# Feed-forward up projection of an attention and feed-forward kernel: eight instead of six of the eleven feature tiles of a pair by seven block products, and rows copied to fp16 by GpSimd

## The reference, cut to what matters

```python
x = x + xattn(layernorm(x), ctx, ...)          # not touched
xq = act_fake_quant(layernorm(x), clip_x)      # whole numbers -128..127 times a scale
gate = einsum('bsh,ih->bsi', xq, weight_fake_quant(w_gate))   # 512 -> 1408
up = einsum('bsh,ih->bsi', xq, weight_fake_quant(w_up))       # 512 -> 1408
h = act_fake_quant(silu(gate) * up, clip_down)
x = x + einsum('bsi,hi->bsh', h, weight_fake_quant(w_down))   # 1408 -> 512
```

## Time and profile before

| | us |
|---|---|
| median of three runs | 1239.04 (1238.58 to 1240.55) |
| the profiled execution | 1239.66 |
| its span in the trace | 1237.9 |
| attention, start to the first feed-forward matmul | 0 to 783.0 |
| groups 0 and 1 | about 789 to 826 |
| the six pairs | about 826 to 1039 |
| groups 14 and 15 | about 1039 to 1078 |
| down projection | about 1082 to the end |

### The profile page before, as it was taken

One profiled execution on the slowest core, in us unless ns is written; L12 is line 12 of the kernel. 1 busy time (PEld: TensorE's weight loads), 2 busy tenths in 40 slices (PEclk: granted clock), 3 DMA queues, 4 the chain that ended last, 5 costly groups with the idle time before them and its releaser, 6 DMA issues.

```text
span 1237.9 us, 20617 instructions
## 1 busy us (share of the span) xinstructions
PE 1230.6 (99%) x7500; PEld 573.2 (46%) x7500; DVE 1052.5 (85%) x1917; ACT 858.5 (69%) x1349; POOL 381.1 (31%) x295
## 2 busy tenths in 40 slices
PE   8999999999999999999999999999999999999998
PEld 5544444444444444444444444544444444444444
DVE  7976988988988898898898868889999998888777
ACT  6888577657757757756765763468888885399760
POOL 0113343144044134224314420224444443022223
PEclk9999999999999999999999999999999999999999
DMA  8284346256254363462462483398976854199996
GB/s 315 86 255 171 95 137 209 66 159 190 79 178 152 111 191 108 120 222 69 137 228 79 119 236 131 139 289 242 278 239 228 272 183 154 47 372 414 423 426 261
DMA packets 174565, 241.74 MB, mean 195 GB/s; under 512 B 122608, under 2 KB 142080, under 8 KB 156928
## 3 DMA queue, kind: packets, MB, share of 16 engines
q1 hardware_dynamic: 174432, 240.42, 58.5%
q10 hardware_dynamic: 32, 0.01, 0.0%
HBM read 120.86 MB, written 90.57 MB: 171 GB/s over the span
## 4 chain that ended last, share of the span: by engine, by line
PE 93%; ACT 3%; DVE 2%; DMA 1%; issue 1%; SPq 1%; ACTq 0%
PE bank L2502 12%; PE po L81 10%; PE po L83 9%; PE po L82 9%; PE bank L2379 8%; PE ring L83 8%; PE ring L82 8%; PE ring L81 8%; PE bank L2384 4%; PE bank L2385 4%; PE bank L2360 3%; PE bank L2341 3%; PE ring L1257 2%; PE ring L1284 2%; DMA x<-in_x_dram 1%; ACT E L479 1%
## 5 line engine op out<-in xcount | busy, mean ns | idle before, releaser
L81 PE MATMUL ring<-yT,M 128*128 128x512 f16 x512 | 194.1, 379 | 0.0
L82 PE MATMUL ring<-yT,M 128*128 128x512 f16 x512 | 194.0, 379 | 0.0
L83 PE MATMUL ring<-yT,M 128*128 128x512 f16 x512 | 194.0, 379 | 0.0
L81 PE MATMUL po<-VW,p 128*128 128x512 f16 x480 | 182.2, 380 | 0.0
L82 PE MATMUL po<-VW,p 128*128 128x512 f16 x480 | 181.9, 379 | 0.0
L83 PE MATMUL po<-VW,p 128*128 128x512 f16 x480 | 181.9, 379 | 0.0
L494 ACT ACTIVATE p<-E 128x512 f16<-128x512 f32 x120 | 74.8, 625 | 122.7 <-DVE E L741 122.7
L414 POOL TENSOR_TENSOR esum<-E 128x512 f32<-128x512 f32 x16 | 23.4, 1462 | 409.2 <-DVE p L745 369.6
L417 POOL TENSOR_TENSOR esum<-esum,E 128x512 f32<-128x512 f32 x96 | 129.5, 1349 | 51.2 <-ACT E L483 18.4
L2502 PE MATMUL bank<-w,hb 128*128 128x512 f16 x605 | 131.3, 379 | 0.0
L1989 ACT ACTIVATE hb<-hb,hscale 128x512 int8<-128x512 f32 (+1 forms) x155 | 95.2, 709 | 16.7 <-DMA hb<-hidden 13.4
(11 more groups left out here) (389 smaller groups left out, 2492.9 us busy)
## 6 DMA issues: line engine op xcount, KB each, us to landing
xa<-x_rows_d SPq DMA_DIRECT2D x28, 1024.0 KB, 6.9
hidden<-hb SPq DMA_DIRECT2D x22, 1024.0 KB, 9.1
hb<-hidden SPq DMA_DIRECT2D x18, 1024.0 KB, 9.8
x<-in_x_dram SPq DMA_DIRECT2D x16, 1024.0 KB, 5.2
value_fold<-E SPq DMA_DIRECT2D x64, 256.0 KB, 2.5
VW<-value_fold SPq DMA_DIRECT2D x16, 1024.0 KB, 6.5
x_rows_d<-x SPq DMA_DIRECT2D x16, 1024.0 KB, 6.0
out_dram<-xa SPq DMA_DIRECT2D x11, 1024.0 KB, 11.6
```

The lines of the kernel that those rows point to most:

```text
L81: nc.tensor.matmul(out, a_hi, b_hi, start=first, stop=False)
L82: nc.tensor.matmul(out, a_hi, b_lo, start=False, stop=False)
L83: return nc.tensor.matmul(out, a_lo, b_hi, start=False, stop=last)
```

## The change

Joint tiles of a pair are now 0, 1, 3, 4, 6, 7, 9, 10, single ones 2, 5, 8. Where two joint tiles follow each other (also from tile 10 to tile 0 of the next pair), `first` and `seed` of the next go ahead of `fourth` of the one at hand (`ahead`). GpSimd copies rows to fp16, one row block at a time (`round_row`), from group 5 on; VectorE's `round_x` is left for groups 1 to 4. Odd groups have a buffer of their own (`xq_odd`). The weight sums are in eight instructions over four tiles each, where there were four over six. The rows to normalise are at other tiles, and VectorE's order in a pair is a new one.

```diff
-    JOINT = tuple(range(0, FT, 2))
+    JOINT = tuple(i for i in range(FT) if i % 3 != 2)
+    SINGLE = tuple(i for i in range(FT) if i % 3 == 2)
     NJ, NS = len(JOINT), FT - len(JOINT)
     ALL_J, ALL_S = NJ * len(PAIRS), NS * len(PAIRS)
-    joint = lambda p, i: NJ * (p - 1) + i // 2
-    TAKEN = ("seed", "third", "silu_a", "fourth", "silu_b")
+    joint = lambda p, i: NJ * (p - 1) + JOINT.index(i)
+    ahead = lambda K: 0 < K < ALL_J and (K % NJ == 0 or JOINT[K % NJ] - 1 in JOINT)
...
+    def order_of_takes():
+
+        taken = []
+        for K in range(ALL_J):
+            if not ahead(K):
+                taken.append(("seed", K))
+            taken.append(("third", K))
+            if K > 0:
+                taken.append(("silu_b", K - 1))
+            taken.append(("silu_a", K))
+            if ahead(K + 1):
+                taken.append(("seed", K + 1))
+            taken.append(("fourth", K))
+        taken.append(("silu_b", ALL_J - 1))
+        return {take: n + 1 for n, take in enumerate(taken)}
+
+    TAKEN = order_of_takes()
+    taken_joint = lambda what, K: TAKEN[what, K]
...
+    BY_POOL = 5
+    xq_of = lambda g: xq_apart if g == 2 else xq_odd if g >= BY_POOL and g % 2 else xq[:]
...
+    xq_odd = spare16[:, SUMS_T + SUMS_W:SUMS_T + SUMS_W + TT * D].rearrange("p (t d) -> p t d", t=TT)
...
+    def rows_of_pair(p):
+
+        early = {6: (2 * p + 4, 0), 9: (2 * p + 4, 3)}
+        late = {1: (2 * p + 3, 1), 3: (2 * p + 3, 2), 4: (2 * p + 3, 3), 6: (2 * p + 4, 1), 7: (2 * p + 4, 2), 9: (2 * p + 5, 0)}
+        if p == 1:
+            early[1] = (2 * p + 3, 0)
+        return [{i: row for i, row in rows.items() if row[0] < NG} for rows in (early, late)]
...
         def turn(g):
-            sp.wait_ge(x_rounded, g)
+            if g < BY_POOL:
+                sp.wait_ge(x_rounded, g)
+            else:
...
+            third_tiles = lambda half, c0, n: half.rearrange("p c (i n) -> p c i n", n=P)[:, c0:c0 + 2, n:FT:3]
+            of_them = lambda k, n: wsum[:, k, :, n:len(JOINT):2]
+            for n in range(2):
+                nc.gpsimd.tensor_tensor(of_them(2, n), third_tiles(wg, 0, n), third_tiles(wu, 0, n), ALU.subtract).then_inc(w_summed, 1)
+                nc.gpsimd.tensor_tensor(of_them(0, n), third_tiles(wu, 0, n), third_tiles(wu, 2, n), ALU.add).then_inc(w_summed, 1)
...
+        def round_row(g, t):
+
+            pool.wait_ge(x_normed, TT * (g - 1) + t + 1)
+            if g > BY_POOL:
+                pool.wait_ge(x_turned[g % 2], 64 * ((g - 1) // 2))
+            nc.gpsimd.tensor_copy(xq_of(g)[:, t], ints_of(g)[:, t]).then_inc(rows_rounded, 1)
+
         over_partitions(0)
         sum_weights()
         for p in PAIRS:
+            early, late = rows_of_pair(p)
             for i in JOINT:
                 add_fourth(p, i)
+                if i in early:
+                    round_row(*early[i])
+                if i in late:
+                    round_row(*late[i])
                 joint_hidden_b(p, i)
...
         for p in PAIRS:
+            early, late = rows_of_pair(p)
             for i in JOINT:
-                seed(p, i)
+                if not ahead(joint(p, i)):
+                    seed(p, i)
                 keep_third(p, i)
+                if i - 1 in SINGLE:
+                    single_silu(p, i - 1, 1)
                 if i > 0:
-                    single_silu(p, i - 1, 1)
-                if joint(p, i) > 0:
-                    joint_silu_b(p if i > 0 else p - 1, i - 2 if i > 0 else JOINT[-1])
-                if p == 1:
-                    early, late = {2: (2 * p + 3, 0), 4: (2 * p + 3, 2)}, {2: (2 * p + 3, 1), 4: (2 * p + 3, 3)}
-                else:
-                    early, late = {2: (2 * p + 3, 1), 4: (2 * p + 3, 3)}, {0: (2 * p + 3, 0), 2: (2 * p + 3, 2)}
-                early.update({6: (2 * p + 4, 0), 8: (2 * p + 4, 2)})
-                late.update({6: (2 * p + 4, 1), 8: (2 * p + 4, 3)})
-                if i in early and early[i][0] < NG:
+                    joint_silu_b(p, JOINT[JOINT.index(i) - 1])
+                elif p - 1 in PAIRS:
+                    joint_silu_b(p - 1, JOINT[-1])
+                if i in early:
                     normalise_row(*early[i])
                 joint_silu_a(p, i)
-                if i < JOINT[-1]:
+                if i + 1 in SINGLE:
                     single_silu(p, i + 1, 0)
-                if i in late and late[i][0] < NG:
+                if i in late:
                     normalise_row(*late[i])
+                if i + 1 in JOINT:
+                    seed(p, i + 1)
+                elif i == JOINT[-1] and p + 1 in PAIRS:
+                    seed(p + 1, 0)
                 keep_fourth(p, i)
...
             if p - 1 in PAIRS:
+                pair_reach(p - 1, 8)
+                joint_hidden_a(p, 0)
                 pair_reach(p - 1, 7)
-                single_hidden(p - 1, 9, 1)
-                joint_hidden_a(p - 1, 10)
+                pair_reach(p - 1, 9)
+            else:
+                joint_hidden_a(p, 0)
+                round_x(4)
+            cross(p, 1)
+            single_hidden(p, 2, 0)
+            if p - 1 in PAIRS:
                 pair_reach(p - 1, 6)
-                cross(p, 0)
-                pair_reach(p - 1, 9)
-            single_hidden(p, 1, 0)
-            joint_hidden_a(p, 0)
-            round_x(2 * p + 2)
+                joint_hidden_a(p, 1)
+                pair_reach(p - 1, 10)
+            else:
+                reach(1, 9)
+                joint_hidden_a(p, 1)
+                reach(1, 10)
+            cross(p, 3)
+            single_hidden(p, 2, 1)
+            pair_reach(p, 0)
+            joint_hidden_a(p, 3)
             if p - 1 in PAIRS:
-                pair_reach(p - 1, 8)
-            single_hidden(p, 1, 1)
-            cross(p, 2)
-            if p - 1 in PAIRS:
-                pair_reach(p - 1, 10)
                 join_pair(p - 1)
             else:
-                reach(1, 9)
-                reach(1, 10)
                 join_group(1)
-            single_hidden(p, 3, 0)
-            joint_hidden_a(p, 2)
             pair_reach(p, 1)
-            pair_reach(p, 0)
-            single_hidden(p, 3, 1)
             cross(p, 4)
-            if p > 1:
-                round_x(2 * p + 3)
-            pair_reach(p, 3)
-            if p == 1:
-                round_x(2 * p + 3)
+            pair_reach(p, 2)
             single_hidden(p, 5, 0)
             joint_hidden_a(p, 4)
-            pair_reach(p, 2)
+            pair_reach(p, 3)
+            cross(p, 6)
             single_hidden(p, 5, 1)
-            cross(p, 6)
             pair_reach(p, 5)
-            single_hidden(p, 7, 0)
             joint_hidden_a(p, 6)
             pair_reach(p, 4)
+            cross(p, 7)
+            single_hidden(p, 8, 0)
+            joint_hidden_a(p, 7)
             if p + 1 in PAIRS:
                 sum_x(p + 1, 0)
                 sum_x(p + 1, 1)
-            single_hidden(p, 7, 1)
-            cross(p, 8)
+            cross(p, 9)
+            single_hidden(p, 8, 1)
             if p + 1 in PAIRS:
                 sum_x(p + 1, 2)
-            single_hidden(p, 9, 0)
-            joint_hidden_a(p, 8)
+            joint_hidden_a(p, 9)
+            cross(p, 10)
             if p + 1 in PAIRS:
                 sum_x(p + 1, 3)
-            cross(p, 10)
-        pair_reach(PAIRS[-1], 7)
-        single_hidden(PAIRS[-1], 9, 1)
-        joint_hidden_a(PAIRS[-1], 10)
-        pair_reach(PAIRS[-1], 6)
+            joint_hidden_a(p, 10)
+            if p + 1 in PAIRS:
+                cross(p + 1, 0)
         for i in range(FT):
+            if i == 1:
+                pair_reach(PAIRS[-1], 9)
             hidden(2, i)
             if i == 0:
-                pair_reach(PAIRS[-1], 9)
-                pair_reach(PAIRS[-1], 8)
+                for m in (8, 7, 6):
+                    pair_reach(PAIRS[-1], m)
             else:
                 reach(2, i - 1)
             if i == 1:
-                pair_reach(PAIRS[-1], JOINT[-1])
+                pair_reach(PAIRS[-1], 10)
             if i == 2:
                 join_pair(PAIRS[-1])
...
             for i in JOINT:
                 if joint(p, i) == 0:
                     pe.wait_ge(x_turned[0], 64 * p)
-                if joint(p, i) == 0 or i > 0:
+                if not ahead(joint(p, i)):
                     joint_first(p, i)
                 joint_third(p, i)
                 if joint(p, i) == 0:
                     up(1, FT - 1, ("up",))
+                if i - 1 in SINGLE:
+                    single_product(p, i - 1, 2)
                 if i > 0:
-                    single_product(p, i - 1, 2)
-                if joint(p, i) > 0:
-                    joint_close(p if i > 0 else p - 1, i - 2 if i > 0 else JOINT[-1])
-                if 0 < i < JOINT[-1]:
-                    single_product(p, i - 1, 3)
+                    joint_close(p, JOINT[JOINT.index(i) - 1])
+                elif p - 1 in PAIRS:
```

(58 more changed lines are left out.)

15 lines of the change are left out of this document (8 added, 7 removed).

## The result

| | before | after |
|---|---|---|
| median us | 1239.55 (1238.58 to 1240.55, 4 runs) | 1252.56 (1251.32 to 1255.72, 4 runs) |
| ratio, 95% interval | | 1.011 (1.0098 to 1.0123) |
| profiled execution, span | 1239.66, 1237.9 | 1255.72, 1253.9 |

The change makes the kernel 13.0 us slower. The profiled execution of after is its slowest, 3.2 us above its median; I come back to that.

A forecast was written before the change was run, and what follows sets the result against it. TensorE, 99% busy, was the bound: matmuls and old gaps removed (-5.2, -0.7) and new waits (6.4, 1.3, 0.7, 2.35, 2.6, 0.75, 1.5) sum to +9.7 us. Forecast 1248.5 us; range 1238 to 1256, own 1244 to 1253.

The forecast's parts named there:

- TensorE as the bound, and the matmuls: TensorE is busy 99% of the span; 160 matmuls a pair instead of 164 save 5.2 us.
- ScalarE's rows in tiles 6 and 9: Two rows ahead of keep_fourth make TensorE's close wait 0.64 us, ten times: 6.4 us.
- Where joint tiles adjoin: Borders between neighbouring joint tiles, where TensorE waits for VectorE's and ScalarE's results; priced place by place.
- Tile 10: first of the next pair waits for joint_silu_b, fourth for cross: 0.25 us, at five borders 1.3 us.
- pair 6: Its tile 10 has no first between second and fourth, so TensorE waits 0.7 us once.
- tile 1: VectorE's two maxima ahead of cross delay TensorE 0.5 us; at five borders 2.6 us.
- Tile 0: GpSimd's two copies delay joint_silu_b of 10; TensorE waits 0.47 us, at five borders 2.35 us.
- rival 3: GpSimd becomes a bound, a copy taking 1.28 us or more: 1255.6 us, chance 0.14.
- The load: Load of group 2p+5 lands after ScalarE wants its first row in tile 9: 0.3 us, five pairs, 1.5 us.
- Pair 1's start: Waits in tile 0 (0.25) and tile 1 (0.5, round_x(4) in the maxima's place): 0.75 us together.
- The first: Rival: the waits do not form and the count of matmuls decides, 1233.2 us; chance 0.14.
- The second: Rival: only ScalarE's rows cost (6.4 us), the other waits are hidden: +0.5, 1239.5 us; chance 0.09.

The follow-up runs named there:

- the first experiment: The changed kernel, but ScalarE normalises row (2p+5, 0) in tile 1 of the next pair instead of tile 9: 1246.59 us, ratio 1.006.
- the three together: The changed kernel with (2p+5, 0) in the next pair's tile 1, (2p+4, 1) behind keep_fourth, tile 9's maximum behind cross: 1242.34 us, ratio 1.0023.
- the copies alone: The kernel before with only GpSimd's row copies to fp16 from group 5 on and a buffer for odd groups: 1241.74 us, ratio 1.0021.
- the casts given back: A version with tile 8's products moved into tiles 9 and 10, VectorE's order mended, but VectorE making all casts, GpSimd none: 1266.51 us, ratio 1.022.

## Why the prediction was right

The measured 1252.56 us lies within the forecast's own range (1244 to 1253), at its upper end and 4.1 us above its point, 1248.5. The mechanism was right; some sizes were not, and two agreed by luck.

**TensorE as the bound, and the matmuls.** Right: 24 matmuls fewer, and the loss and the gain of every version is read as waits of TensorE.

**ScalarE's rows in tiles 6 and 9.** 6.4 forecast, 6.2 measured, and the two experiments that move one row each take the wait to 0.10. That rests on rows of before alone: differences of starts on one engine could be added up over seven instructions to 0.01 us.

**Where joint tiles adjoin.** Tile 10 1.3 (1.35), pair 6 0.7 (0.71), tile 1 2.6 (2.2: the chain to `fourth` is 4.22 for 4.18, but a close of 0.10 already delays TensorE on its side). Tile 0 2.35 (1.7). Its chain came out: from `keep_fourth` of 9 (899.18) to `joint_silu_b` of 10 (904.09) are 4.91 us, forecast 4.9. But TensorE waits 0.33 and not 0.45: the forecast added 0.12 for the close's own latency to a wait that covers it.

That two copies take 1.67 us there (901.06 to 902.73), for 1.6 forecast, is luck. A copy alone takes 0.61 and lets the next start after 0.55; two of those would by the forecast's own sum (up to 0.63 each) have made nothing wait. The second takes 1.15, beside a `sum_x`, and a price for GpSimd and VectorE getting in each other's way is what the forecast had put at nothing. GpSimd's copies into one of the two buffers (count, then minimum, median, maximum in ns; the other 20 have 604/612/1075):

```profile
L1886 POOL CAST hb<-xa x24: 607/614/1158, 836.7 to 1039.0; 128x512 f16<-128x512 int8 x24
```

The forecast took 0.8, between the bounds 0 and 1.28.

The Trainium skill, GPSIMD Engine Reference, section "Engine selection", with its one-input work roughly at line rate, gave an estimate of 0.43 for it; the trace has 0.61 alone, nearly half as much again, and a mean of 0.73.

Made twice, the copies make TensorE wait 1.80 us at a border: that is rival 3's mechanism, at the length of copies it needed (1.28). At their own length they cost next to nothing there: with one copy less in the first experiment, 0.33 of the 0.40 us stayed, since `cross` of tile 0 then makes TensorE wait.

**The load: the term that was mis-sized.** 0.3 us in five pairs was forecast, 1.5; the profiled execution has 4.8 in three. The timeline of SyncE, of the first pair and of the fourth:

```profile
847.01 6.47 SPq L1734 DMA_TRANSPOSE xqT<-hb  x4
853.53 0.58 SPq L1716 DMA_DIRECT2D xa<-x_rows_d  x1
...
961.98 5.12 SPq L1734 DMA_TRANSPOSE xa<-hb  x4
967.15 0.58 SPq L1716 DMA_DIRECT2D xa<-x_rows_d  x1
```
```profile
860.65 0.81 ACT L1927 ACTIVATE xa<-xa,row_bias,rowq 128x512 int8<-128x512 f32 x1 [1.33 <-DMA xa<-x_rows_d]
...
975.90 0.81 ACT L1927 ACTIVATE xa<-xa,row_bias,rowq 128x512 int8<-128x512 f32 x1 [1.62 <-DMA xa<-x_rows_d]
```

In the first pair four turns take 6.47 instead of 5.12, and the load lands 7.1 after its issue. In the fourth the turns are as before, and the load takes 8.75 (in the third 8.6), beside DMA engines at a share of 1.01. In the second and the fifth pair it takes 7.0 and 6.9, at shares of 0.85 and 0.87, and lands 0.1 to 0.2 us before ScalarE wants it. The stretches of the second and the fourth pair, the DMA share last but one:

```profile
890.00:900.00 10.00, 9.54 (x45) 4.16 (x44) 8.19 (x11) 8.96 (x16) 7.04 (x8) 1.00 0.85 264
967.00:977.00 10.00, 8.59 (x40) 3.72 (x38) 7.40 (x10) 7.55 (x13) 6.12 (x7) 1.00 1.01 310
```
So the place was priced right to 0.5 us where the load takes its usual time. I had put one value each, 5.17 and 7.0, where the trace of before gave only a median; a wait behind two DMAs needs their spread. At its median the kernel is 3.2 us better than in this execution. That this wait and the clock behind it make the difference is argued only: the versions without the load's wait spread over 1.7 us (the first experiment) and 2.4 (the three together), after over 4.4, but with the copies made twice, where the load is late in all five pairs, the four runs lie within 0.5. Taken so, load and clock cost 6.5 - 3.2 = 3.3 us at the median for the 1.5 forecast. These 1.8 more, 2.9 for the places left out (below) and some 1.3 less at tile 0, tile 1 and `keep_fourth` make 3.4; the medians differ by 3.3 more than forecast (13.0 for 9.7).

**Left out.** 0.10 at each close (1.2), which the same sums would have given had I gone past tiles 6, 9 and 10, and 0.17 at `cross` of tile 4 (1.0), gone in the version whose maxima stand behind the crosses. Pair 1's start cost 1.45 for 0.75: TensorE waits 0.35 for the turn of group 3, 0.35 for the first `sum_x`, which had waited 1.4 us for that turn, and 0.75 for the fourth `sum_x`, which stands behind `cross` of tile 0. That the last equals the forecast's 0.75 is luck: that was 0.25 and 0.5 for the crosses of tiles 0 and 1, and the one of tile 1 cost 0.10.

**The rivals.** The first (no waits, 1233.2) is out; even the best order measured leaves 4.5 us of waits. The second (only ScalarE) leaves out 2.2 us of maxima and the borders, which the experiments take away one by one. The third's mechanism is real, but the wait is 0.33 us and not 1.3.

## What to carry to other kernels

When TensorE is the bound with no slack, price a new order by adding up differences of starts on each engine, from a matmul to the one that waits for its result; that foretold ten waits to 0.02 us each. Do the same for every place where the order changed, not only for those that look tight, and for a wait that stands behind DMAs take the spread of their times, not the median alone. To move a product, move its readers too: two of the misses among the experiments were a reader left where it was, and long instructions put ahead of a short one that TensorE waited for. The other two (the copies alone, the casts given back) were turns and loads that moved with the copy ahead of them.
